# Routing a gated cross-attention block with experts: counts by TensorE, tile places by partition, expert weights split ahead of the last FFN pieces

## The chip, the cores and the metric

One core of one Trainium2 chip runs the whole program. The metric is the device time of one execution in microseconds (us), lower is better; of the kernel before three runs are given, and one profiled execution.

## What is computed

The input `x` has 32 samples of 256 tokens with 256 features, the context 32 times 77 tokens. Cut to what matters:

```python
x = x + tanh(g_xattn) * (attention(layernorm(x), ctx, ctx) @ W.T + b)      # 16 heads of 16, causal, softmax over 77
flat = layernorm(x)                                                        # 8192 tokens
shared = swiglu(flat @ w_in.T) @ w_out.T                                   # hidden 512
g_idx = argmax(flat @ wg.T + gb)                                           # 2 groups
masked = where(group of expert == g_idx, flat @ we.T + eb, -inf)           # 4 experts of that group
topv, topi = top_k(softmax(masked) * g_prob, 2)
routed = sum over the two: (swiglu(flat @ w1.T) * topv) @ w2[topi].T
x = x + tanh(g_ffn) * (shared + routed)
```

## The kernel before

A token's two experts lie in one group of four, so there are 2 x 6 = 12 pairs, called classes. **Phase one** goes over the samples: attention, the shared FFN and, from the logits, each token's class, its two weights and its place among the tokens of its class. GpSimd scatters a record (token, two weights) to that place in a table in DRAM (`tab`); the residual and the normed row go to `y` in DRAM. **Phase two** takes the table in tiles of 128 tokens of one class (`NTILE` = 76 at most, in chunks of four): GpSimd gathers their rows of `y`, TensorE transposes them, computes the hidden layer and multiplies it with the class's two experts, picked by a register; VectorE adds, GpSimd scatters the result.

The order of work is one Python list (`phase_one()`), which every engine's program walks through in the same sequence, emitting only its own part. Each iteration `i` has 12 slots into which the attention stages of several samples are put. Behind each slot come pieces of the shared FFN: a chunk of two samples has 24, of which 0 to 15 compute the hidden layer (four blocks: two pieces for `ha`, two for `hb`) and 16 to 23 the output, in halves `so`; pieces 19 and 23 end in `res`, which SyncE writes to `y`. Behind each FFN piece come pieces of a route. `ROUTES` lists nine: seven of eight tiles, two of four. A route of eight tiles has 63 pieces before: 55 for VectorE (each a small operation that waits for the one ahead) and 8 scatters for GpSimd. On the way a running count per class (`Cc`) is made tile by tile, and TensorE turns it and the one-hot classes (`OH`) into each token's rank (`rank`, L647 and L648).

TensorE's results go to rings of PSUM banks (`take`): the FFN and the rank share ring F with two banks in phase one and get ring B with all eight from `phase_two` on. A bank is free when its reader has counted a semaphore (`freed`): `u` and `f` for the hidden pieces, `res` for the output, `roh` (VectorE's product of rank and one-hot) for the rank. In hidden blocks ScalarE makes a tanh and a rounded copy `gh`, VectorE `u` (L1149) and `f` (`gf`, L1157), GpSimd the remainder `gl` (L1358), for which the output pieces wait.

At the end of phase one, `tiles` computes for each of the 76 tiles where it begins in the table (`ti`) and its experts (`ei`), on one partition of VectorE in 24 pieces (L1255 to L1289). `split_w2` turns the expert weights, loaded by SyncE in 16 halves into six buffers of `Pt`, into a rounded part (ScalarE) and a remainder (VectorE for even, GpSimd for odd halves), and issues the load that comes next. `records` has SyncE read a tile's place into a register and fetch its 128 records. `gather` has GpSimd fetch rows of `y`; it waits until all of `y` is written (`yr0`, `yr1`, `yn0`, `yn1`).

```python
            while at["ffn"] < (12 * (i - 5) + slot - 5) // 2 * 2:
                ...
                for _ in range(2 if i < NB else 3):
                    route()
```

Of the kernel before, what the change touches and what calls it, by code (L numbers as in the profile page):

```python
# [29 lines left out]
NCH = NB // 2  # L30


DCON = {n: i + 1 for i, n in enumerate(
    "idb ks0 kb0 ones rec pre_zero pre zero_row va_zero va_one wgh0 wgl0 tgh brow pbias".split())}
GCON = {n: i + 6 for i, n in enumerate("ident caus cauT upb".split())}
# [4 lines left out]
R_EXP1, R_EXP2, R_RANK = 3, 9, 30  # L40


def route_pieces(r):
    return R_RANK + 17 + 2 * ROUTES[r][1]
# [6 lines left out]
def phase_one():  # L51
# [15 lines left out]
    for i in range(NB + 4):  # L67
# [19 lines left out]
        for slot in range(12):  # L87
# [17 lines left out]
    n = w = tiles = 0  # L105
    while at["ffn"] < 24 * NCH:
        for _ in range(4):
            if at["r"] < len(ROUTES):
                route()
            elif tiles < 24:  # L110
                order.append(("tiles", 0, tiles))
                tiles += 1
        if n >= 4 and w < 2 * NE:
            order.append(("split_w2", w, 0))
            w += 1
        order.append(("ffn", at["ffn"] // 24, at["ffn"] % 24))
        at["ffn"] += 1
        n += 1
    while at["r"] < len(ROUTES):
        route()  # L120
    while tiles < 24:
        order.append(("tiles", 0, tiles))
        tiles += 1
# [6 lines left out]
def build(nc, A, out):  # L130
    ctx = ExitStack()
    with ctx:
# [3 lines left out]
            "xT mm mTp sc val O aT pj x2T lg lgt ha hb so rank tot z ha2 hb2 ex "  # L136
# [21 lines left out]
        def freed(use):  # L158
# [8 lines left out]
                "so": lambda: (s["res"], 2 * n + k + 1), "rank": lambda: (s["roh"], n + 1), "tot": lambda: (s["tv"], 1),  # L167
# [25 lines left out]
        Cc = sb("Cc", [P, 9, NC], BF)  # L193
# [4 lines left out]
        def carve(rows, shape, of=w2a):  # L198
# [61 lines left out]
        tb = sb("tb", [P, 2, 2, 512])  # L260
        tt, bt = tb[:, 0, :, :], tb[:, 1, :, :]
# [5 lines left out]
        LG = sb("LG", [P, 4, 4, 10])  # L267
        upb = sb("upb", [P, P], BF)
        io12 = sb("io12", [P, NC])
        l4 = sb("l4", [P, 8, 4])  # L270
        ge4 = sb("ge4", [P, 8, 4])
        s4t = sb("s4t", [P, 8, 4])
        c6 = sb("c6", [P, 8, 6])
        R1 = sb("R1", [P, 8, 8])
# [7 lines left out]
        half = NB // 2 * K  # L282
        mk_s = [v.bitcast(I32).rearrange("p (b k) -> p b k", k=K) for v in (
            af[:, 4736:4736 + half], tb[:, :, :, :].rearrange("p a b n -> p (a b n)")[:, 0:half])]
# [1184 lines left out]
```

## Time and profile before

| | |
|---|---|
| median of 3 runs | 1304.08 us (1302.39 to 1304.59) |
| the profiled execution, its own time | 1309.0 us |
| its span in the profile | 1307.2 us |
| TensorE busy | 1155.2 us (88% of the span) |
| VectorE busy | 865.0 us (66%) |
| GpSimd busy | 549.1 us (42%) |
| ScalarE busy | 505.8 us (39%) |
| mean granted TensorE clock | 0.969 of full speed |

Busy is the time in which an engine executes; an engine with 88% has some 150 us in which it does nothing, and the profile says for each such gap on whom it waited. In the profile's timelines and groups PE is TensorE, DVE VectorE, ACT ScalarE, POOL GpSimd, and SPq the DMA issues of SyncE. The granted clock is a share of 2.4 GHz; 0.5 is its lower level, 1.2 GHz.

### The profile page before, as it was taken

How to read it: one execution, taken by the hardware profiler on the slowest of the kernel's cores; microseconds unless marked ns; L12 is line 12 of the kernel's file. 1: busy time of each engine (PE TensorE's matmuls, PEld its weight loads, DVE VectorE, ACT ScalarE, POOL GpSimd, SP SyncE). 2: the span in 40 equal slices, each digit the busy share in tenths (PEclk: the TensorE clock that was granted, in tenths of full speed). 3: DMA queues.
4: the chain of work that ended last, by engine and by line, in shares of the span. 5: the costliest groups of instructions: out<-in, count | busy, mean ns of one | idle time of the engine just before them, and what ended most of it. 6: DMA issues, size and time to landing. Idle time of an engine off the chain costs nothing.

```text
span 1307.2 us, 22394 instructions
## 1 busy us (share of the span) xinstructions
PE 1155.2 (88%) x7387; PEld 918.4 (70%) x7387; DVE 865.0 (66%) x1968; ACT 505.8 (39%) x780; POOL 549.1 (42%) x658
## 2 busy tenths in 40 slices
PE   1688999998999999999999985179999999999997
PEld 0356777776777777777767764168888888888886
DVE  4455687687577777876876776546666566666665
ACT  3355555454455545554554423122222222222220
POOL 2122334326126235334342345345556556555543
PEclk9998999999999999999999988689999999999999
DMA  4756464645446355544635114323222222122210
GB/s 153 137 110 124 104 131 79 115 109 97 90 104 119 82 112 114 105 92 111 129 70 99 43 33 121 106 51 75 64 66 68 66 69 70 62 69 73 63 34 10
DMA packets 108263, 115.30 MB, mean 88 GB/s; under 512 B 36942, under 2 KB 88433, under 8 KB 108148
## 3 DMA queue, kind: packets, MB, share of 16 engines
q1 hardware_dynamic: 96376, 85.41, 31.6%
q0 software_dynamic: 11776, 28.46, 7.3%
q8 instruction: 64, 1.05, 0.4%
q14 instruction: 47, 0.39, 0.1%
HBM read 50.44 MB, written 28.64 MB: 60 GB/s over the span
## 4 chain that ended last, share of the span: by engine, by line
PE 64%; DVE 16%; issue 5%; POOL 4%; SPq 4%; DMA 3%; ACT 2%; POOLq 0%; DVEq 0%; ACTq 0%
PE ps L681 15%; PE ps L699 11%; PE ps L618 6%; PE ps L702 5%; PE ps L635 5%; PE ps L526 4%; PE ps L541 4%; PE ps L572 2%; PE ps L502 2%; DMA w2a<-w2a 2%; PE ps L497 2%; PE ps L594 2%; DVE mneg L1093 2%; PE ps L550 1%; DVE gf L1157 1%
## 5 line engine op out<-in xcount | busy, mean ns | idle before, releaser
L699 PE MATMUL ps<-w2a,gh 128*128 x608 | 218.5, 399 | 0.0
L759 ACT ACTIVATE Pt<-ps,pbias 77x1024 f32<-77x1024 f32 x128 | 142.1, 1110 | 103.3 <-PE ps L528 102.2
L702 PE MATMUL ps<-w2a,gl 128*128 x608 | 170.5, 280 | 0.0
L1411 POOL DMA_INDIRECT out<-ot,Pt x76 | 78.4, 1032 | 153.0 <-DVE ot L1232 149.6
L1303 POOL TENSOR_SCALAR ve<-mv 128x2 f32<-128x2 f32 x64 | 15.5, 242 | 284.7 <-DVE mv L882 284.0
L699 PEld LDWEIGHTS ps<-w2a,gh 128*128 128x128 f32 x608 | 114.2, 188 | 25.1
L1093 DVE TENSOR_REDUCE mneg<-ps 128x8 f32<-128x616 f32 x128 | 101.5, 794 | 44.6 <-PE ps L502 44.4
L681 PE MATMUL ps<-z2h,w1h 128*128 128x512 f32 x304 | 121.8, 401 | 8.3 <-DVE z2l L886 8.3
L1358 POOL TENSOR_TENSOR gl<-gf,gh 128x512 fp32r<-128x512 f32 x64 | 83.0, 1297 | 109.6 <-ACT gh L801 109.5
L526 PE MATMUL ps<-w2a 100*77 100x256 f32 x512 | 106.5, 324 | 22.9 <-DMA w2a<-w2a 17.9
L855 ACT ACTIVATE tt<-ps 128x512 f32<-128x512 f32 x76 | 45.4, 597 | 198.5 <-PE ps L681 198.5
L681 PE MATMUL ps<-z2l,w1h 128*128 128x512 f32 x304 | 120.5, 397 | 0.0
L681 PE MATMUL ps<-z2h,w1l 128*128 128x512 f32 x304 | 120.4, 396 | 0.0
L702 PEld LDWEIGHTS ps<-w2a,gl 128*128 128x128 f32 x608 | 114.5, 188 | 1.5
L618 PE MATMUL ps<-x2h,winh 128*128 128x512 f32 x256 | 112.7, 440 | 1.5 <-DVE gf L1157 1.3
L1397 POOL TENSOR_TENSOR gl<-gf,gh 128x512 fp32r<-128x512 f32 x76 | 98.5, 1297 | 16.4 <-ACT gh L859 14.5
L635 PE MATMUL ps<-woh,gh 128*128 128x256 f32 x256 | 79.9, 312 | 25.2 <-POOL gl L1358 25.1
L618 PE MATMUL ps<-x2h,winl 128*128 128x512 f32 x256 | 101.4, 396 | 0.0
L618 PE MATMUL ps<-x2l,winh 128*128 128x512 f32 x256 | 100.8, 394 | 0.0
L859 ACT ACTIVATE gh<-gf 128x512 fp32r<-128x512 f32 x76 | 48.0, 632 | 126.8 <-DVE gf L1215 126.8
L1210 DVE SCALAR_TENSOR_TENSOR uu<-tt,ps 128x512 f32<-128x512 f32 x76 | 52.2, 687 | 62.4 <-ACT tt L855 62.4
L526 PEld LDWEIGHTS ps<-w2a 100*77 100x77 f32 x512 | 64.2, 156 | 34.4 <-issue 21.1
(205 smaller groups left out, 2763.4 us busy)
## 6 DMA issues: line engine op xcount, KB each, us to landing
w2a<-w2a SPq DMA_DIRECT2D x96, 256.0 KB, 5.9
af<-in_x SPq DMA_DIRECT2D x32, 256.0 KB, 3.5
x<-in_x SPq DMA_DIRECT2D x32, 256.0 KB, 7.1
y_dram<-xn SPq DMA_DIRECT2D x32, 256.0 KB, 3.6
y_dram<-res SPq DMA_DIRECT2D x32, 256.0 KB, 2.4
w2a<-w2a SPq DMA_DIRECT2D x96, 77.0 KB, 2.8
Pt<-in_w2T SPq DMA_DIRECT2D x16, 256.0 KB, 3.5
af<-in_ctxT SPq DMA_DIRECT2D x16, 154.0 KB, 3.0
```

Source lines behind the costliest of these rows:

```text
L526: e.matmul(bk[0:K, j * S:(j + 1) * S], Kst[:, ks, j, p % 4, 2 * g + p // 4, :], Xs[:, h, p % 4, p // 4, :], start=j == 0, stop=False, skip ...
L541: m = e.matmul(bk[32 * j:32 * j + 32, q * S:(q + 1) * S], Vau[:, ks, g, n, :], Pt[0:K, n, :], start=True, stop=True)
L618: m = e.matmul(bk[:, :], w[:, cc, off:off + P], x[:, b % 2, cc, :], start=cc == 0 and n == 0, stop=cc == 1 and n == 2)
L635: m = e.matmul(o[:, t, :], x[:, fc, at:at + P], w[:, fc, :], start=fc == 0 and t == 0 and n == 0, stop=fc == 3 and n == 2, skip_group_chec ...
L681: m = e.matmul(bk[:, :], w[:, cc, off:off + P], x[:, c % 2, cc, :], start=n == 0, stop=n == 5)
L699: e.matmul(o, gh2[:, c % 2, fc, t * P:(t + 1) * P], w2v[:, bass.ds(val, 1), fc, :, :].rearrange("p o h d -> p (o h) d"), start=fc == 0, st ...
L702: m = e.matmul(o[:, 0, :], gl2[:, c % 2, fc, t * P:(t + 1) * P], w2v[:, bass.ds(val, 1), fc, 0, :].rearrange("p o d -> p (o d)"), start=Fa ...
L759: e.activation(Pt[0:K, 4 * k:4 * k + 4, :].rearrange("k (n j) t -> k n (j t)", n=2), bank_of["sc", b, k][0:K, :, :], ACT.Exp, bias=pbias[: ...
L1093: e.tensor_reduce(mneg[:, h, t, :].rearrange("p (j q c) -> p c j q", j=2, c=2)[:, c], bank_of["mm", b, k][:, :, 0:4 * K].rearrange("p q (f ...
L1358: e.tensor_tensor(gl[:, fc - 1, :], gf[:, n % 2, :], gh[:, fc - 1, :].bitcast(F), ALU.subtract).then_inc(s["gl"], 1)
L1397: e.tensor_tensor(gl2[:, c % 2, fc, :], gf2[:, fc % 2, :], gh2[:, c % 2, fc, :].bitcast(F), ALU.subtract).then_inc(s["gl2"], 1)
L1411: e.indirect_dma_start(out.rearrange("b s d -> (b s) d"), bass.IndirectOffsetOnAxis(ap=rt[:, k, 0:1].bitcast(I32), axis=0), ot[:, k % 8, : ...
```

## The change

- A route has 30 pieces for VectorE (32 instructions but for shared copies) and its scatters. Both groups' experts are compared at once (`cmp`, 4 x 4 comparisons per group) and masked by group (`gm`). The running count is one vector per route (`carry`, two buffers).
- The counts of tiles within a route are TensorE's: the rank sum gets one matmul of ones with the one-hot classes for each distance between tiles, one with the carry, one with the class's start in the table (`crow`), 10 matmuls for eight tiles and 6 for four.
- `tiles` has three pieces, with a tile on each partition: a matmul gives the totals per class (T1), one the running sum of tiles (T2), and three transposes (T3) bring place and experts back to one row.
- FFN pieces come nine slots later; one route piece stands behind each up to iteration 30, three after that. The scatters so get one FFN piece each.
- The first six loads of `w2` stand at the end of iteration 33 (`load_w2`), 12 of 16 splits in iteration 35, the last four among pieces 8 to 11 of the last FFN chunk.
- `sel` is gone; its numbers come with `io12`. The mask is loaded in parts of 19 and 13 samples. `LG` is split into `LGg` and `LGe`.

```diff
-            while at["ffn"] < (12 * (i - 5) + slot - 5) // 2 * 2:
+            while at["ffn"] < (12 * (i - 5) + slot - 14) // 2 * 2:
                 order.append(("ffn", at["ffn"] // 24, at["ffn"] % 24))
                 at["ffn"] += 1
-                for _ in range(2 if i < NB else 3):
+                for _ in range(1 if i < NB - 1 else 3):
                     route()
+            if i == NB + 3:
+                order.append(("split_w2", slot, 0))
+        if i == NB + 1:
+            order.append(("load_w2", 0, 0))
...
     order.append(("phase_two", 0, 0))
-    n = w = tiles = 0
+    n, w, k = 0, 12, 0
     while at["ffn"] < 24 * NCH:
-        for _ in range(4):
-            if at["r"] < len(ROUTES):
-                route()
-            elif tiles < 24:
-                order.append(("tiles", 0, tiles))
-                tiles += 1
-        if n >= 4 and w < 2 * NE:
-            order.append(("split_w2", w, 0))
-            w += 1
+        for _ in range(3):
+            route()
         order.append(("ffn", at["ffn"] // 24, at["ffn"] % 24))
         at["ffn"] += 1
         n += 1
+        if at["r"] == len(ROUTES) - 1 and at["k"] > R_RANK + 3 or at["r"] == len(ROUTES):
+            if n % 2 == 0 and k < 3:
+                order.append(("tiles", 0, k))
+                k += 1
+            elif k == 3 and w < 2 * NE:
+                order.append(("split_w2", w, 0))
+                w += 1
...
-                elif stage_ == "route" and k == R_RANK + ROUTES[b][1] + 6:
+                elif stage_ == "route" and k == R_RANK:
...
-                    e.matmul(bk[:, 0:J * NC], upb[:, :], OH[:, 0:J, :].rearrange("p j c -> p (j c)"), start=True, stop=False)
-                    e.matmul(bk[:, 0:J * NC], onesb[:, :], Cc[:, 0:J, :].rearrange("p j c -> p (j c)"),
-                             start=False, stop=True).then_inc(s["rank"], 1)
+                    o = OH[:, 0:J, :].rearrange("p j c -> p (j c)")
+                    e.matmul(bk[:, 0:J * NC], upb[:, :], o, start=True, stop=False, skip_group_check=True)
+                    for d in range(1, J):
+                        e.matmul(bk[:, d * NC:J * NC], onesb[:, :], o[:, 0:(J - d) * NC], start=False, stop=False,
+                                 skip_group_check=True)
...
+                elif stage_ == "tiles":
+                    bk, (sem, v) = take("B", ("T1", "T2", "T3")[k], 0, 0)
+                    e.wait_ge(sem, v)
+                    if k == 0:
+
+                        e.wait_ge(s["rcc"], len(ROUTES))
+                        e.matmul(bk[0:NC, 0:P], carry[:, len(ROUTES) % 2, :], onesb[:, :], start=True, stop=True).then_inc(s["T1"], 1)
+                    elif k == 1:
+
+                        e.wait_ge(s["nt"], 3)
+                        e.matmul(bk[:, 0:NC], ntb[:, :], upb[0:NC, 1:NC + 1], start=True, stop=True).then_inc(s["T2"], 1)
+                    else:
+                        e.wait_ge(s["tk"], 7)
+                        for n in range(3):
+                            m = e.transpose(bk[0:1, n * P:(n + 1) * P], tk[:, n:n + 1], ident[:, :])
+                        m.then_inc(s["T3"], 1)
...
-                for j in range(J):
-                    after()
-                    step(e.tensor_tensor(Cc[:, j + 1, :], Cc[:, j, :], OH[:, j, :], ALU.add), *(("rcc", r + 1) if j == J - 1 else ()))
+                step(e.tensor_reduce(ct[:, :], oh.rearrange("p j c -> p c j"), AX, ALU.add))
+                yield
+                after()
+                step(e.tensor_tensor(carry[:, (r + 1) % 2, :], ct[:, :], carry[:, r % 2, :], ALU.add), "rcc", r + 1)
```

What moves, at three places. First TensorE in the third route, at the rank sum (L647 and L648 before, L662 to L669 now; L618 and L631 are hidden pieces of the FFN, L635 and L648 of the change output pieces). Before:

```order
L618 MATMUL ps<-x2h,winl 128x512
L647 MATMUL ps<-OH,upb 128x96 [waits s_rcc,s_u]
L648 MATMUL ps<-Cc,onesb 128x96
L618 MATMUL ps<-x2h,winh 128x512
L618 MATMUL ps<-x2l,winh 128x512
L618 MATMUL ps<-x2h,winl 128x512
```

Now:

```order
L648 MATMUL ps<-woh,gl 128x256
L662 MATMUL ps<-OH,upb 128x96 [waits s_rcc,s_f]
L664 MATMUL ps<-OH,onesb 128x84
L664 MATMUL ps<-OH,onesb 128x72
L664 MATMUL ps<-OH,onesb 128x60
L664 MATMUL ps<-OH,onesb 128x48
L664 MATMUL ps<-OH,onesb 128x36
L664 MATMUL ps<-OH,onesb 128x24
L664 MATMUL ps<-OH,onesb 128x12
L666 MATMUL ps<-carry,onesb 128x96
L669 MATMUL ps<-crow,onesb 128x96
L648 MATMUL ps<-woh,gh 128x256 [waits s_gl]
```

The two sums have become ten matmuls, and stand between the output pieces 16 and 17, no longer in the middle of a hidden block.

Second, TensorE again, where the bank of that rank sum is next wanted (`s_roh` is VectorE's reading of it; L497 and L510 are score tiles of `max`). Before, in the next block of the same route's stretch:

```order
L526 MATMUL ps<-w2a 77x256 [waits s_mt0,s_P,s_xs0,s_kd0]
L526 MATMUL ps<-w2a 77x256
L528 MATMUL ps<-cauT,identb 77x2x77
L526 MATMUL ps<-w2a 77x256 x2
L528 MATMUL ps<-cauT,identb 77x2x77
L618 MATMUL ps<-x2h,winh 128x512 [waits s_roh]
L618 MATMUL ps<-x2l,winh 128x512
L618 MATMUL ps<-x2h,winl 128x512
```

Now, seven FFN pieces behind the sum, at the next chunk's piece 0:

```order
L541 MATMUL ps<-cauT,identb 77x2x77
L539 MATMUL ps<-w2a 77x256 x2
L541 MATMUL ps<-cauT,identb 77x2x77
L510 MATMUL ps<-w2a 128x308 [waits s_att]
L510 MATMUL ps<-w2a 128x308
L515 MATMUL ps<-pad,identb 128x308 x2
L631 MATMUL ps<-x2h,winh 128x512 [waits s_roh,s_x2l]
L631 MATMUL ps<-x2l,winh 128x512
```

The wait for `roh` has moved from behind the scores to right behind the score tiles of `max`, at hidden piece 0 of a chunk.

Third, VectorE at the end of phase one (`res` is the last FFN result, L1181 and L1186 splits, `w1l` the beginning of phase two). Before:

```order
L1181 TENSOR_TENSOR w2a<-Pt,w2a 128x2x256 [waits s_wh]
L1279 TENSOR_TENSOR Pt<-Pt 1x76 [waits s_tv]
L1280 TENSOR_TENSOR af<-af,Pt 1x912
L1282 TENSOR_REDUCE Pt<-af 1x76 [waits s_tv]
L1284 CAST af<-Pt 1x76 [waits s_tv]
L1285 TENSOR_TENSOR af<-af,Pt 1x912
L1287 TENSOR_REDUCE Pt<-af 1x76 [waits s_tv]
L1167 SCALAR_TENSOR_TENSOR res<-ps,tg,x 128x512 [waits s_yr1,s_x1,s_so]
L1289 TENSOR_SCALAR af<-Pt 1x76 [waits s_tv]
L1181 TENSOR_TENSOR w2a<-Pt,w2a 128x2x256 [waits s_wh]
L1196 TENSOR_TENSOR w1l<-Pt,w1h 128x4x128 [waits s_yn1,s_yn0,s_scat,s_yr1,s_wh,s_yr0,s_gl]
```

Now:

```order
L1287 TENSOR_SCALAR af<-ps 1x76
L1186 TENSOR_TENSOR w2a<-Pt,w2a 128x2x256 [waits s_wh]
L1154 SCALAR_TENSOR_TENSOR tt<-tt,ps 128x512 [waits s_t]
L1186 TENSOR_TENSOR w2a<-Pt,w2a 128x2x256 [waits s_wh]
L1162 TENSOR_TENSOR gf<-tt,ps 128x512 [waits s_gl,s_hb,s_u]
L1154 SCALAR_TENSOR_TENSOR tt<-tt,ps 128x512 [waits s_t]
L1162 TENSOR_TENSOR gf<-tt,ps 128x512 [waits s_gl,s_hb,s_u]
L1172 SCALAR_TENSOR_TENSOR res<-ps,tg,x 128x512 [waits s_yr0,s_x1,s_so]
L1172 SCALAR_TENSOR_TENSOR res<-ps,tg,x 128x512 [waits s_yr1,s_x1,s_so]
L1201 TENSOR_TENSOR w1l<-Pt,w1h 128x4x128 [waits s_yn1,s_yn0,s_scat,s_yr1,s_wh,s_yr0,s_gl]
```

The tile steps, now L1258 to L1287, end before the last two splits, and behind those only FFN rows are left; between the last two `res` there is nothing.

## Rows read from the trace of the kernel before

**Rows 1.** Windows, two steady iterations: PE, PEld, DVE, ACT, POOL busy, clock, DMA share, GB/s

```profile
446.10:466.30 20.20, 19.26 (x148) 14.66 (x146) 17.92 (x53) 11.98 (x20) 6.59 (x11) 1.00 0.52 116
490.10:511.80 21.70, 19.85 (x150) 14.89 (x148) 16.70 (x36) 11.92 (x19) 16.06 (x22) 1.00 0.56 114
```

**Rows 2.** Windows, the join of the two phases

```profile
750.00:770.00 20.00, 17.13 (x99) 14.07 (x98) 16.76 (x53) 5.57 (x11) 9.92 (x10) 1.00 0.06 16
770.00:780.00 10.00, 6.47 (x33) 5.71 (x32) 7.47 (x28) 1.23 (x2) 2.36 (x4) 0.67 0.15 52
...
790.00:800.00 10.00, 3.28 (x15) 2.35 (x13) 9.35 (x36) 4.49 (x10) 4.05 (x4) 0.87 0.27 81
800.00:810.00 10.00, 5.73 (x27) 4.94 (x27) 8.65 (x31) 4.94 (x10) 4.28 (x5) 0.79 0.53 167
810.00:820.00 10.00, 5.25 (x30) 5.05 (x30) 3.62 (x6) 1.89 (x3) 8.98 (x8) 0.66 0.40 93
...
870.00:880.00 10.00, 8.53 (x32) 6.98 (x33) 4.90 (x9) 3.04 (x6) 3.84 (x3) 0.71 0.07 2
```

**Rows 3.** Timeline of PE: start, us, engine, line, instruction, [idle before <-releaser]

```profile
800.19 0.20 PE L647 MATMUL ps<-OH,upb 128*128 128x48 bf16 x1 [6.92 <-DVE Cc L998]
...
814.60 0.58 PE L635 MATMUL ps<-woh,gh 128*128 128x256 f32 x1 [8.67 <-POOL gl L1358]
...
819.57 0.28 PE L635 MATMUL ps<-woh,gl 128*128 128x256 f32 x1
...
849.89 0.79 PE L681 MATMUL ps<-z2h,w1h 128*128 128x512 f32 x1 [1.41 <-DVE z2l L886]
...
871.47 0.79 PE L681 MATMUL ps<-z2h,w1h 128*128 128x512 f32 x1 [6.85 <-DVE z2l L886]
```

**Rows 4.** Timeline of POOL in the same stretch

```profile
812.05 1.27 POOL L1379 TENSOR_TENSOR w2a<-Pt,w2a 128x512 fp32r<-128x512 f32 x1
...
839.34 1.11 POOL L1294 DMA_INDIRECT af<-y_dram,Pt  x1 [19.85 <-DMA Pt<-tab_dram]
...
862.45 1.03 POOL L1294 DMA_INDIRECT yt<-y_dram,Pt  x1 [10.97 <-DMA Pt<-tab_dram]
```

**Rows 5.** Timeline of DVE: four route steps, a tile step, the last res

```profile
799.29 0.76 DVE L998 TENSOR_TENSOR Cc<-Cc,OH 128x12 bf16<-128x12 bf16 x4
...
821.12 1.10 DVE L1268 TENSOR_TENSOR af<-Pt 1x912 f32<-1x912 f32 x1
...
831.04 0.73 DVE L1167 SCALAR_TENSOR_TENSOR res<-ps,tg,x 128x512 f32<-128x512 f32 x1
```

**Rows 6.** Timeline of SyncE's DMA issues, merged

```profile
783.30 34.16 SPq L367 DMA_DIRECT2D Pt<-in_w2T  x16
...
831.80 0.38 SPq L439 DMA_DIRECT2D y_dram<-res  x1
833.44 46.01 SPq L378 DMA_DIRECT2D Pt<-tab_dram  x41
```

**Rows 7.** Timeline of ACT, its first row of phase two

```profile
834.21 0.63 ACT L841 ACTIVATE w1h<-Pt 128x512 fp32r<-128x512 f32 x1 [13.21 <-DMA y_dram<-res]
```

**Rows 8.** Windows, iterations 4 and 5, at the start of phase one

```profile
85.20:105.40 20.20, 13.22 (x106) 8.89 (x106) 10.26 (x25) 9.15 (x14) 3.84 (x8) 0.89 0.75 159
105.40:125.30 19.90, 19.37 (x136) 14.83 (x136) 11.67 (x26) 11.19 (x17) 4.96 (x9) 0.94 0.52 102
```

**Rows 9.** Chain that ended last: start, us; one hidden piece

```profile
781.71 1.38 PE ps L618 x6
```

**Rows 10.** By line: duration ns min/median/max, first and last start, forms

```profile
L647 PEld LDWEIGHTS ps<-OH,upb x9: 95/95/105, 206.6 to 800.2; 128*128 128x128 bf16 x9
...
L989 DVE TENSOR_TENSOR OH<-R,io x9: 207/247/257, 191.2 to 798.3; 128x96 bf16<-128x96 f32 x7, 128x48 bf16<-128x48 f32 x2
```

**Rows 11.** The page's groups: busy us, mean ns | idle before, releaser

```profile
L1093 DVE TENSOR_REDUCE mneg<-ps 128x8 f32<-128x616 f32 x128 | 101.5, 794 | 44.6 <-PE ps L502 44.4
```

**Rows 12.** Groups of PE from 100 to 700 us, same columns

```profile
L526 PE MATMUL ps<-w2a 100*77 100x256 f32 x428 | 86.1, 316 | 15.1 <-DMA w2a<-w2a 11.0 <-DVE mneg L1093 3.7 <-ACT Pt L759 0.4
```

More of the change, by code:

```diff
@@ L118, in phase_one @@
         n += 1
+        if at["r"] == len(ROUTES) - 1 and at["k"] > R_RANK + 3 or at["r"] == len(ROUTES):
[5 more added lines that the diff above has]
+                w += 1
     while at["r"] < len(ROUTES):
         route()
-    while tiles < 24:
-        order.append(("tiles", 0, tiles))
-        tiles += 1
+    order += [("tiles", 0, x) for x in range(k, 3)]
     order.append(("gather", 0, 0))
@@ L457, in sync @@
                         load_w(b + 6)
-                elif stage_ == "tiles" and k == 23:
+                elif stage_ == "tiles" and k == 2:
                     e.wait_ge(s["ti"], 1)
@@ L650, in tensor @@
+                    e.matmul(bk[:, 0:J * NC], onesb[0:1, :], crow[:, 0:J * NC], start=False, stop=True,
+                             skip_group_check=True).then_inc(s["rank"], 1)
                 elif stage_ == "phase_two":
                     ffn_ring = "B"
-                elif stage_ == "tiles" and k == 0:
-                    bk, (sem, v) = take("B", "tot", 0, 0)
+                elif stage_ == "tiles":
+                    bk, (sem, v) = take("B", ("T1", "T2", "T3")[k], 0, 0)
                     e.wait_ge(sem, v)
-                    e.wait_ge(s["rcc"], len(ROUTES))
-                    e.matmul(bk[:, 0:NC], onesb[:, :], Cc[:, ROUTES[-1][1], :], start=True, stop=True).then_inc(s["tot"], 1)
+                    if k == 0:
[9 more added lines that the diff above has]
+                        m.then_inc(s["T3"], 1)
@@ L927, in route @@
                 yield
                 after()
[L929 removed]
+                step(e.tensor_tensor(m_.rearrange("p t i j -> p t (i j)"), m_.rearrange("p t i j -> p t (i j)"), each(tri, T),
+                                     ALU.mult))
                 yield
                 after()
[L932 removed]
+                step(e.tensor_reduce(r_, m_, AX, ALU.add))
+                yield
+                step(e.tensor_reduce(c_, m_.rearrange("p t i j -> p t j i"), AX, ALU.add))
@@ L1019, in route @@
-                oh = OHR[:, 0:J, :]
-                step(e.tensor_tensor(oh, bank_of["rank", r, 0][:, 0:J * NC].rearrange("p (j c) -> p j c", c=NC), o, ALU.mult),
-                     "roh", r + 1)
-                yield
-                after()
-                step(e.tensor_reduce(col(5), oh, AX, ALU.add))
-                yield
+                for n, op in enumerate((ALU.is_lt, ALU.is_ge)):
+                    after()
+                    step(e.scalar_tensor_tensor(lh[:, :, n, :], by8(r_), 0.5, by8(e_), op, ALU.mult))
+                    yield
```

301 lines of the change are left out of this document (137 added, 164 removed), and 2 rows, old and new, of the table names.

## The prediction

> **What bounds the kernel now.** I read the busy time of the engines by stretch first, then TensorE's timeline where it is not full, then the timelines of the engines it waits for there. Phase one (attention, shared FFN and routing, to about 820 us) and phase two (the experts) both keep TensorE busy: two steady iterations of phase one show 19.26 of 20.20 us and 19.85 of 21.70 us [rows 1]. From 890 us to the end it is full, and the change touches nothing there. What is left is the join. From 750 to 820 us TensorE is idle for 2.87 + 3.53 + 6.72 + 4.27 + 4.75 = 22.1 us [rows 2]: most is a wait of 6.9 us for VectorE's class counts and one of 8.7 us for GpSimd's `gl` [rows 3], which stood behind record scatters and an expert split (`w2a` at 812.05) [rows 4]. The granted clock falls after such stops. Busy time times the missing share of the clock gives 6.5 x 0.33 + 3.3 x 0.13 + 5.7 x 0.21 + 5.3 x 0.34 = 5.6 us lost [rows 2]. Then comes the hole: the last FFN matmul starts at 819.6, the first hidden matmul of phase two at 849.9, 30.3 us later [rows 3]. In it VectorE works through the tile table on one partition in steps of 1.1 us, and the last `res` (done by the same engine) starts at 831.0 though its input was ready at 819.9 [rows 5]. SyncE writes it at 831.8, fetches records from 833.4 at 46.0 / 41 = 1.1 us each [rows 6], ScalarE sees the row landed at 834.2 [rows 7], GpSimd gathers from 839.3 [rows 4], and 10.6 us later TensorE is at work. Last, a stop of 6.9 us before 871.5 [rows 3], because the gathers of the third chunk wait for 24 records (862.5) and the `gl` of phase two stands behind them [rows 4].
>
> **The join after the change.** The order puts the end of routing, the three `tiles` pieces and the last four splits ahead of FFN piece 12 of the last chunk. Behind that only FFN work is left on VectorE and GpSimd. The eight records of the first two chunks are also fetched before the last `res`. So from the last FFN matmul on: 0.1 us to `res`, 3.2 us from its start to landed (831.04 to 834.21) [rows 5, 7], some 0.4 us to the gather, 10.6 us from gather to first hidden matmul [rows 3, 4]. That makes 14.3 us against 30.3: **-16.0 us**. Next is late the third chunk: SyncE starts its 16 records 1.6 us after the last `y` write (831.8 to 833.4), about 2.5 us behind the last matmul, so they are landed at 2.5 + 16 x 1.1 + 1.7 = 22 us; in the old run 9.0 us passed from that gather to TensorE (862.45 to 871.47) [rows 3, 4, 6]: 31.5 us. TensorE had run 14.7 us on its own before the old stop (871.5 - 6.9 - 849.9) [rows 3], so it now stops at 14.3 + 14.7 = 29.0 and waits 2.5 us instead of 6.9. The clock lost behind the old stop was 8.5 x 0.29 = 2.5 us [rows 2], of which I give back 2. Together **-6.4 us**.
>
> **The tail of phase one.** The 22.1 idle and 5.6 clock go, and new waits come, which I add as one term. TensorE waits in the last route for the counts (18 VectorE steps of 0.19 us and up [rows 5], with two `res` between, against 5.6 us of its own pieces): 2 to 4 us. T2 and T3 each want VectorE's answer after two FFN pieces (2.8 us): 2.5 together. `gl` of piece 19 is due 3.1 us after piece 15 and covered by 2.2 us: 1 each in chunks 14 and 15. Chunk 14 has splits in front of its `gl`: 2. I take **+10 us**, ends 4 and 22 (the last is what stands there now). Sum for the tail: **-17.7 us**.
>
> The splits themselves (12 in the last iteration of phase one) add per piece one ScalarE copy and half a split each on VectorE and GpSimd. They cost nothing while TensorE has a piece of 1.4 us beside each. The cover would be gone if the loads came no faster than the old 34.16 / 16 = 2.1 us each [rows 6]; those were paced by the order, not by the queue.
>
> **What it costs elsewhere.** (1) FFN pieces are issued nine slots later. Iterations without FFN take no less time: 20.2 us (85.2 to 105.4) with 13.2 busy, the next, with six pieces, 19.9 us with 19.4 busy [rows 8]. The filling starts later: by the end of iteration 6 the old order has 18 pieces out, the new 8. Eight of the ten missing are hidden pieces of 1.38 us [rows 9] and two are output pieces with half the columns, 0.7 us: 12.4 us of work falls out of a stretch with room into one without: **+12.4 us**. The bounds are 0 (iterations shorten as much) and 14. (2) Nine rank sums take 10 matmuls (6 for four tiles) for 2: 64 more, with at most 96 columns. From below they cost next to nothing, 1 us; from above the weight load, 95 ns each [rows 10], is 6 us. I take **+3**. The Trainium skill (TensorE: Matmul & The Clock Gate, "Back-to-back issue gap") gives about 81 ns for each pair of weight load and matmul with 128 columns; by that the term would be 5 us, and no row here times a run of such pairs.
>
> (3) The bank. Phase one has two banks for FFN and rank. Before, the rank sum was freed one route step after it was made. Now TensorE makes it at route piece 20, VectorE reads it at piece 28 (`roh`), one piece per FFN piece, so the hidden piece 0 of the next chunk waits for `s_roh`, just behind the score tiles of `max`. VectorE must first reduce those (0.79 us) [rows 11], then do the product (0.26 by the 96-element step) [rows 10]: 1.1 us in each of six routes, **+6.6**. (4) Against that the eight scatters of a route now stand one behind each FFN piece, no longer two. The iteration with scatters idles 1.85 us, the one without 0.94 [rows 1]: seven times 0.9 is **-6.4**. The queries' DMA before the scores gets a light or heavy pair more beside it; waits for it in the steady part are 11.0 us in all [rows 12], of which I take **-3**. VectorE loses about 23 instructions in a route of eight tiles and gains seven bigger ones: worth nothing, since it is not what the steady part waits for.
>
> **Sum.** -16.0 - 6.4 - 17.7 + 12.4 + 3 + 6.6 - 6.4 - 3 = -27.5 us. The profiled execution took 1309.0 us, so it would be 1281.5; the median of the runs is 1304.1, which gives **1277 us**.
>
> **Rivals.**
> A, the above: 0.53, from 1268 to 1284.
> B, the tail gives half of it back: splits and tanh share ScalarE with only two banks, or the records delay the last `y` write (SyncE must fetch eight of them, 8.8 us, after the last scatter has landed, and has only about 11 us of matmuls for it). For: GpSimd's scatters held everything up here before. Against: eight pieces without any side work follow. The tail term rises from 10 to 22, giving 1289. Chance 0.20.
> C, steady iterations gain too (idle 0.9 instead of 1.4 on average over 25 iterations, from scatters, lighter VectorE and better cover of the queries' DMA): about 13 us more, 1264. For: VectorE is 17.9 of 20.2 us busy there. Against: TensorE is 95% busy. Chance 0.17.
> D, slower: the bank of (3). VectorE is not just one reduction behind at piece 28 but also behind `klo`, which waits for ScalarE and a load, and each wait is long enough to bring the clock down. At 5 us of wait and 2 of clock, six times, the term is 42 for 6.6, giving 1312. It decides from 34 / 6 = 5.7 us per wait. For: it is a true wait with nothing of TensorE's that can pass it. Against: in the old trace VectorE is some 0.6 us behind at that slot. Chance 0.06.
> E, no change: the hole moves. The later filling (12.4), the bank and a tail as bad as before cancel what the hole gives, 1300 to 1306. The code does move the work, so this needs several at once: 0.04.
>
> **Numbers.** The likeliest case gives 1277. A reaches from 1268 to 1284, B above to 1292, C below to 1260: the range 1261 to 1291 leaves out about 2 in 10. Faster or slower counts beyond 0.2% (2.6 us, about what runs of this kernel can tell). Faster 0.90 (A, B, C), same 0.04 (E), slower 0.06 (D).
>
> **What would show it.** The last FFN matmul some 5 us earlier than 820; 14 to 15 us from there to the first hidden matmul, with the `y` write right behind `res`; the stop in phase two below 4 us; in the last route single waits below 4 us; FFN starting in the iteration that begins at 125 us with about 12 us more idle before; six waits of TensorE of about 1 us for `OHR`. I am wrong if waits for `OHR` are 4 us or more, if iterations before the first FFN piece get shorter than 19 us, or if `y` is written 3 us or more after `res`.

## The result and the profile after

The changed kernel took 1299.55 us (median of 20 runs, 1292.18 to 1306.12), the kernel before beside it 1306.2 us: ratio 0.9943, interval 0.9926 to 0.996. It is faster by some 7 us; 1277 was forecast, and the measured time lies above the forecast's 1261 to 1291. The profiled execution took 1304.0 us, span 1302.3.

The page of the changed kernel, busy time by engine and the granted clock in 40 slices:

```profile
PE 1157.2 (89%) x7455; PEld 918.1 (70%) x7455; DVE 814.9 (63%) x1767; ACT 502.4 (39%) x780; POOL 549.3 (42%) x659
...
PEclk9998999999999999999999998889999999999999
```

VectorE has 50 us less to do, TensorE as much as before. The join by windows (columns as in [rows 2]), with the two steady windows of [rows 1] at the end:

```profile
750.00:770.00 20.00, 19.23 (x147) 15.80 (x147) 9.18 (x23) 9.93 (x14) 13.91 (x15) 1.00 0.09 27
770.00:780.00 10.00, 7.97 (x58) 6.65 (x57) 9.02 (x34) 2.12 (x5) 0.94 (x2) 0.99 0.82 241
...
800.00:810.00 10.00, 5.94 (x29) 5.49 (x30) 8.53 (x16) 4.56 (x9) 7.67 (x6) 0.68 0.74 240
810.00:820.00 10.00, 8.53 (x45) 6.10 (x43) 8.31 (x34) 2.23 (x4) 1.14 (x1) 0.98 0.27 79
...
840.00:850.00 10.00, 1.08 (x4) 0.72 (x4) 0.74 (x1) 0.63 (x1) 4.93 (x5) 0.56 0.55 156
870.00:880.00 10.00, 10.00 (x52) 8.27 (x52) 5.39 (x10) 3.29 (x6) 4.86 (x5) 1.00 0.11 17
446.10:466.30 20.20, 19.23 (x163) 15.37 (x162) 12.77 (x36) 9.20 (x16) 5.66 (x10) 1.00 0.51 106
490.10:511.80 21.70, 18.16 (x158) 13.92 (x158) 12.38 (x37) 8.35 (x13) 5.47 (x10) 1.00 0.50 101
```

TensorE's timeline at the hole, against [rows 3]: the last FFN matmul, the first hidden one of phase two, the second stop.

```profile
836.62 0.28 PE L648 MATMUL ps<-woh,gl 128*128 128x256 f32 x1
848.92 1.09 PE L699 MATMUL ps<-ident,af 128*128 128x128 f32 x4 [12.02 <-DMA af<-y_dram,Pt]
...
854.51 0.80 PE L713 MATMUL ps<-z2h,w1h 128*128 128x512 f32 x1 [1.41 <-DVE z2l L918]
...
869.48 0.50 PE L713 MATMUL ps<-z2h,w1h 128*128 128x512 f32 x1 [1.07 <-DVE z2l L918]
```

The hole is 854.51 - 836.62 = 17.9 us (30.3 before), the second stop 1.1 (6.9). Yet the last FFN matmul starts 17.1 us later than before. Cut at four marks, both profiled executions:

| stretch | before | after | forecast | measured |
|---|---|---|---|---|
| start to ScalarE's norm of sample 31 | 691.6 | 709.65 | +0.2 | +18.0 |
| from there to the last FFN matmul | 128.0 | 127.0 | -5.3 | -1.0 |
| hole | 30.3 | 17.9 | -16.0 | -12.4 |
| first hidden matmul to the end | 457.3 | 447.8 | -6.4 | -9.5 |

In the first row, rank sums, bank, scatters and queries were put at +3 + 6.6 - 6.4 - 3 = +0.2; the second has 12.4 - 17.7. The miss is in the iterations, which took 18 us longer although some 12 us of FFN work had left them. What TensorE waited for there, 100 to 700 us (engine, line, releaser: us in total, times, longest). Before:

```profile
PE ps L635 <- POOL gl L1358: 11.1, 10, 1.5
PE ps L526 <- DMA w2a<-w2a: 11.0, 6, 5.2
PE ps L497 <- DVE mneg L1093: 10.0, 18, 0.8
PE ps L526 <- DVE mneg L1093: 3.7, 12, 0.4
```

After:

```profile
PE ps L563 <- ACT Pt L791: 17.2, 25, 1.0
PE ps L631 <- DVE OHR L1038: 13.9, 6, 2.3
PE ps L539 <- DMA w2a<-w2a: 11.8, 6, 6.0
PE ps L585 <- ACT af L798: 9.8, 25, 0.4
```

The waits for `gl` and for the maxima are gone; in their place stand one for ScalarE's exp and one for its copy ahead of the projection, 25 times each, and one for the rank's bank, 13.9 us where 6.6 were forecast. In all TensorE is idle for 55.3 us of these 600, before for 37.1. Timeline of PE in one iteration:

```profile
454.55 0.23 PE L541 MATMUL ps<-cauT,identb 77*77 77x154 bf16 x1
454.71 0.41 PE L510 MATMUL ps<-w2a 64*128 64x308 f32 x2
455.05 0.45 PE L515 MATMUL ps<-first,identb 128*128 128x308 bf16 x2
456.07 1.06 PE L563 MATMUL ps<-ident,af 128*128 128x128 f32 x8 [0.58 <-ACT Pt L791]
```

The transposes of attention (L563, slot 2) want the bank that the exp of the scores (slot 1) empties. The two FFN pieces that an iteration issues together are called a pair here. With `slot - 5` the pairs stood behind the odd slots, so one lay between scores and transposes; with `slot - 14` they stand behind the even ones, and none does. The same holds for values (slot 9) and projection (L585, slot 10). The shift by nine changed the parity, which the forecast didn't see.

### The profile page after: what moved, and what is told of

Its sections match the earlier page's. It is cut to its first block, busy times and chain, and to the rows that moved or that the text cites. A ratio compares the mean times of both kernels' runs of the same rounds, so it can differ in the third digit from the quotient of the medians.

```text
span 1302.3 us, 22338 instructions
## 1 busy us (share of the span) xinstructions
PE 1157.2 (89%) x7455; PEld 918.1 (70%) x7455; DVE 814.9 (63%) x1767; ACT 502.4 (39%) x780; POOL 549.3 (42%) x659
## 4 chain that ended last, share of the span: by engine, by line
PE 73%; ACT 6%; issue 5%; DVE 5%; SPq 5%; DMA 4%; POOL 2%; POOLq 0%; ACTq 0%; DVEq 0%
PE ps L713 15%; PE ps L731 11%; PE ps L631 10%; PE ps L648 6%; PE ps L734 6%; PE ps L539 4%; PE ps L554 4%; PE ps L585 3%; DMA w2a<-w2a 3%; PE ps L563 3%; ACT Pt L791 3%; PE ps L515 2%; PE ps L510 2%; PE ps L607 2%; PE ps L541 1%
## 5 line engine op out<-in xcount | busy, mean ns | idle before, releaser
L631 PE MATMUL ps<-x2h,winh 128*128 128x512 f32 x256 | 112.2, 438 | 15.3 <-DVE OHR L1038 13.9
L1301 POOL TENSOR_SCALAR ve<-mv 128x2 f32<-128x2 f32 x64 | 15.2, 237 | 254.7 <-DVE mv L914 254.3
L539 PE MATMUL ps<-w2a 100*77 100x256 f32 x512 | 99.1, 310 | 19.8 <-DMA w2a<-w2a 18.9
L1396 POOL TENSOR_TENSOR gl<-gf,gh 128x512 fp32r<-128x512 f32 x76 | 98.6, 1298 | 14.7 <-ACT gh L891 13.0
L631 PE MATMUL ps<-x2h,winl 128*128 128x512 f32 x256 | 102.1, 399 | 0.0
L631 PE MATMUL ps<-x2l,winh 128*128 128x512 f32 x256 | 101.5, 397 | 0.0
L1374 POOL DMA_INDIRECT tab_dram<-rec,slot x64 | 65.7, 1026 | 58.6 <-issue 56.2
```

The source lines that it names most:

```text
L539: e.matmul(bk[0:K, j * S:(j + 1) * S], Kst[:, ks, j, p % 4, 2 * g + p // 4, :], Xs[:, h, p % 4, p // 4, :], start=j == 0, stop=False, skip ...
L631: m = e.matmul(bk[:, :], w[:, cc, off:off + P], x[:, b % 2, cc, :], start=cc == 0 and n == 0, stop=cc == 1 and n == 2)
L1374: e.indirect_dma_start(tab, bass.IndirectOffsetOnAxis(ap=slot[:, j:j + 1], axis=0), rec[:, j, :], None, bounds_check=NC * NT - 1, oob_is_e ...
L1396: e.tensor_tensor(gl2[:, c % 2, fc, :], gf2[:, fc % 2, :], gh2[:, c % 2, fc, :].bitcast(F), ALU.subtract).then_inc(s["gl2"], 1)
```

## The experiments

The versions were timed in four groups, each on another chip and beside the kernel before, to which all ratios refer. Its median was 1310.8 us in the first group (the four below up to changed_odd_slots) and 1306.3 to 1307.6 in the others, so a difference between versions of two groups is better taken from the ratios; where that matters both are given. Odd and even name the slots that the pairs stand behind.

### The parity of the FFN slots

**before_even_slots**

```diff
-            while at["ffn"] < (12 * (i - 5) + slot - 5) // 2 * 2:
+            while at["ffn"] < (12 * (i - 5) + slot - 6) // 2 * 2:
```

> The kernel before with nothing changed but the shift of the FFN pieces, six slots instead of five, which puts its pairs behind even slots. Theory P: waits for ScalarE's exp (Pt) and its copy ahead of the projection appear in each iteration, some 0.6 and 0.4 us, over 32 iterations 15 to 30 us; time 1318 to 1335. Rival F: one slot less of filling is worth at most 2 us; 1306 to 1308.

1326.6 us, ratio 1.010 (1.006 to 1.014): 16 us slower. The waits appear, the first of them twice as long as expected (29.3 us in 25 waits):

```profile
PE ps L550 <- ACT Pt L759: 29.3, 25, 2.6
PE ps L572 <- ACT af L766: 11.1, 25, 1.0
```

**before_later_even** (`slot - 14` in the kernel before)

> The kernel before with the shift of the changed one (14 slots instead of 5) and nothing else of it. Some 12 us of FFN work move behind the last iteration, where before has 37 us of idle; if they all fill idle time the later filling costs nothing by itself. Theory P: the parity adds 15 to 30 us to the iterations and the tail gives nothing extra back; 1315 to 1330. Rival F: 1300 to 1308.

1340.3 us, 1.022 (1.018 to 1.025): 29.5 us slower, more than theory P's upper end. The same two waits stand in each iteration:

```profile
PE ps L550 <- ACT Pt L759: 18.0, 25, 1.0
PE ps L572 <- ACT af L766: 17.9, 25, 2.6
```

By the marks of the table above, the norm of sample 31 starts 30.5 us later (722.1), the last FFN matmul another 25.0 us later behind it (153.0 for 128.0), and the hole shrinks by 15.5 us (14.8 for 30.3).

**before_later_odd** (`slot - 13`)

> The kernel before with a shift of 13 slots, later by eight as the changed kernel nearly is, but on odd slots as before. Theory P: 15 to 25 us below the same kernel with 14 slots; against the kernel before between no change and 10 us faster (the displaced work fills the 30.3 us hole at the join), 1296 to 1306. Rival F: as with 14 slots, within 2 us.

1290.5 us, 0.983 (0.980 to 0.987). One slot between these two kernels makes 50 us, more than theory P said. And this one number alone, in the kernel before, is worth more than the whole change: the norm of sample 31 starts at 671.1, 20.5 us earlier; the last FFN matmul comes 22.0 us later behind it; the hole shrinks from 30.3 to 14.75 us, since VectorE's tile steps now lie beside FFN work. Of the 20.5 us, 17.0 lie between samples 8 and 31, where each iteration has six pairs in both kernels: the waits for `gl` (11.1 us) are gone there. After the hole:

```profile
835.80 0.80 PE L681 MATMUL ps<-z2h,w1h 128*128 128x512 f32 x1 [1.41 <-issue]
```

**changed_odd_slots** (`slot - 13` in the changed kernel)

> The changed kernel with its FFN pieces eight slots later than before instead of nine, so that pairs stand again behind the odd slots (1, 3, 5, 7, 9, 11) of an iteration and not behind the even ones. Theory P (parity): in the changed kernel PE's transposes of the attention weights (L563) wait 17.2 us and its projections (L585) 9.8 us in 100 to 700 us for ScalarE, 25 times each, because no pair stands between scores and transposes, nor between values and projection; with pairs there both waits go almost wholly, and the time is 15 to 27 us below the changed kernel's 1299.6, near 1280. Rival F (later filling alone): the 12 us that the iterations lost against before come from nine slots of FFN work that are not there in iterations 5 and on, and parity is nothing: 1299 to 1301. Rival R: the waits go, but PE then meets the next late thing of each iteration (max, DMA rows of maxT), and only 3 to 8 us are won.

1332.8 us, 1.016 (1.013 to 1.020): slower by 33 us than on even slots (29 by the ratios), against theory P and its rivals. The two waits for ScalarE did go, but others grew:

```profile
PE ps L539 <- DMA w2a<-w2a: 16.1, 7, 5.8
PE ps L631 <- DVE OHR L1038: 14.6, 5, 3.4
PE ps L595 <- DVE xn L1136: 12.0, 5, 2.4
```

The waiting is 48 us, less than the 55 on even slots; what is lost is clock: 0.94 from 100 to 400 and from 400 to 700 us, where the changed kernel has 0.96 and 1.00. Of stops of 1.5 us and more there are 14 here, and the granted clock is below 1.00 in the 3 us behind 13 of them; the changed kernel has seven, with a lower clock behind two. Behind one of them, PE's timeline and the window (clock is the third number from the end):

```profile
316.89 0.77 PE L631 MATMUL ps<-x2h,winh 128*128 128x512 f32 x1 [3.26 <-DVE OHR L1038]
317.46 0.63 PE L631 MATMUL ps<-x2l,winh 128*128 128x512 f32 x1
```

```profile
316.00:322.00 6.00, 5.11 (x16) 3.42 (x16) 2.25 (x6) 0.60 (x1) 0.35 (x2) 0.50 0.21 60
```

The matmuls take 0.63 us (0.39 otherwise): the clock is at its lower level. The Trainium skill (TensorE: Matmul & The Clock Gate, "Part 1: The HAM clock gate") has the clock fall when TensorE has been idle; this row agrees. How long a stop is does not settle it here: of the six waits of 2.3 us in the changed kernel one was followed by the lower clock in its first profile, and three in the profile of changed_once_more, the same program.

### The rank's bank

**changed_product_early**: VectorE's product, which frees the bank, six steps earlier.

```diff
+                e.wait_ge(s["rank"], r + 1)
+                e.tensor_tensor(OHR[:, 0:J, :], bank_of["rank", r, 0]..., oh, ALU.mult).then_inc(s["roh"], 1)
+                yield
                 after()
                 step(e.tensor_tensor(e_, e_, s_, ALU.mult))
...
-                e.wait_ge(s["rank"], r + 1)
-                step(e.tensor_tensor(OHR[:, 0:J, :], bank_of["rank", r, 0]..., oh, ALU.mult), "roh", r + 1)
-                yield
-                after()
+                e.wait_ge(s["roh"], r + 1)
                 step(e.tensor_reduce(cl[:, 0:J], OHR[:, 0:J, :], AX, ALU.add))
```

> The changed kernel (14 slots, even) with VectorE's product of the rank bank and the one-hot (L1038) six steps earlier, right behind the rank sums. Theory Q (the bank): the wait of 2.3 us at L631 that comes once with each of the six eight-tile routes of iterations 8 to 28 goes, and with it the half-speed clock behind it; 6 x 2.3 = 14 us of waiting and some 3 to 6 us of clock, so 1280 to 1288 against the 1299.6 of the changed kernel. Rival W: the FFN piece then waits for something else that is late at the same place (the copy of its own gate, the weights of attention), and 5 us or less are won.

1281.0 us, 0.9813 (0.979 to 0.984): 18.6 us below the changed kernel (17 by the ratios), as theory Q has it. The wait is gone, the others stay:

```profile
PE ps L563 <- ACT Pt L791: 18.6, 26, 1.0
PE ps L585 <- ACT af L798: 10.2, 26, 0.4
PE ps L539 <- DMA w2a<-w2a: 9.9, 6, 6.0
```

From sample 8 to 31 it needs 518.4 us for 536.1: 17.7, the 13.9 of waiting and 3.8 more, which fits the clock of 0.83 from 315 to 335 us, around the second stop. Why 2.3 us and not 1.1 shows VectorE's queue of the changed kernel ahead of one product:

```profile
506.30 0.48 DVE L1079 TENSOR_TENSOR w2a<-af,w2a 128x308 fp32r<-128x308 f32 x1 [0.78 <-ACT w2a L761]
506.70 0.79 DVE L1097 TENSOR_REDUCE mneg<-ps 128x8 f32<-128x616 f32 x1
507.41 0.25 DVE L1038 TENSOR_TENSOR OHR<-ps,OH 128x96 f32<-128x96 f32 x1
```

```profile
507.80 0.47 PE L631 MATMUL ps<-x2h,winh 128*128 128x512 f32 x1 [2.32 <-DVE OHR L1038]
```

The remainder of the keys (L1079, rival D's `klo`) waits 0.78 us for ScalarE and takes 0.48, then the maxima: 1.1 us more in front of the product than counted.

**changed_odd_product_early**: both edits.

> The changed kernel with its FFN pieces behind odd slots (13) and the product early. On odd slots, without the early product, the profile showed once with each eight-tile route a wait of 2.3 to 3.4 us for the product (L631 for DVE L1038) and one of 2.4 us for the normed rows (L595 for DVE xn, which waits for GpSimd's root behind the scatters), and a clock of 0.94. Theory Q: the first of the two goes, 15 to 20 us of waiting and half of the lost clock; 1332.8 falls to 1305 to 1315. Theory C (the rare long stops cost through the clock, the short ones of each iteration nothing but themselves): the same, and the clock between 100 and 700 us rises from 0.94 to 0.96 or 0.97. Rival: the clock stays at 0.94 whatever stops are left; then over 1315.

1290.3 us, 0.9867 (0.984 to 0.989): 42 us below the same slots without it (38 by the ratios), more than theory Q said, clock 0.97 in both halves. On odd slots the wait for the normed rows (L595, 9.7 us) and the DMA's (17.5) are left.

### How the routing is spread

**changed_odd_early_two_steps**

```diff
-                for _ in range(1 if i < NB - 1 else 3):
+                for _ in range(2 if i < NB - 1 else 3):
                     route()
```

> As the run on odd slots with the product early, and with two steps of routing to an FFN piece instead of one, as the kernel before has it; the eight scatters of a route then lie within four FFN pieces, not eight. Theory S: the wait for the normed rows (L595) came from GpSimd's root standing behind single scatters that were spread over the slots 7 to 11; with the scatters together it is gone in most routes, and with both long stops gone the time is that of the kernel before with 13 slots (1290.5 beside 1310.8 of before, 0.983) less the 10 us of the shorter join; 1270 to 1285. Rival: with two steps to a piece the product has half the distance from the rank sums, or VectorE's steps crowd out the maxima; 1290 to 1310.

1279.8 us, 0.9808 (0.978 to 0.983).

**changed_even_early_two_steps** (the same with `slot - 14`)

> The run with the product early and two steps of routing to an FFN piece (1279.8 on odd slots), now on even slots (14). Nothing but the parity differs. Theory P: the waits for ScalarE between scores and transposes and ahead of the projection (18.6 and 10.2 us in 100 to 700 us of the even run with one step) come back and nothing else goes; 1300 to 1310. Rival G (the parity only exchanges one set of late work for another: on odd slots PE is ahead of the maxima and of the DMA rows, on even slots of ScalarE): 1278 to 1288. With one step to a piece even was 9 us faster than odd.

1294.8 us, 0.9922 (0.989 to 0.995): between what theory P and rival G gave. The waits for ScalarE did come back (19.3 and 10.2 us), and the parity is worth 15 us here. On even slots one step is better by 13.8 (with two, GpSimd's `gl` is late behind pairs of scatters: 8.6 us of waits), on odd slots two by 10.5 (8 by the ratios; with one, the scatters stand among GpSimd's square roots, and the normed rows are late). The spread and the parity can't be valued apart.

**changed_scatters_behind_root**. In the odd run with two steps TensorE still waits twice for the normed rows around the last samples. PE, then POOL, whose eight scatters (six ahead of the root at L1301 and L1303) hold it up:

```profile
725.91 1.08 PE L595 MATMUL ps<-ident,xn 128*128 128x128 f32 x4 [5.32 <-DVE xn L1136]
...
769.40 1.09 PE L595 MATMUL ps<-ident,xn 128*128 128x128 f32 x4 [7.12 <-DVE xn L1136]
```

```profile
716.30 1.13 POOL L1374 DMA_INDIRECT tab_dram<-rec,slot  x1 [1.51 <-DVE slot L1044]
...
722.83 0.97 POOL L1374 DMA_INDIRECT tab_dram<-rec,slot  x1 [0.30 <-issue]
723.81 0.26 POOL L1301 TENSOR_SCALAR ve<-mv 128x2 f32<-128x2 f32 x1
```

```diff
+        if at["k"] == R_SCAT and at["d"] < {6: 8, 7: 8}.get(r, 0):
+            at["d"] += 1
+            return
...
     while at["ffn"] < 24 * NCH:
-        for _ in range(3):
+        for _ in range(5):
             route()
```

> As the run on odd slots, product early, two steps; and the scatters of the last two routes inside the iterations start only behind GpSimd's root of the attention norm (they stood ahead of it; PE's transposes L595 waited 5.3 us at 725.9 and 7.1 us at 769.4 for the rows normed with it), with five steps instead of three to a piece behind the last iteration, so that the last route isn't later. Theory S: both waits go, 12 us, part of it given back at the join if that is bound by the last scatters; 1268 to 1275. Rival: the join is bound by the records that follow the last scatters and by the last FFN rows; what PE wins earlier it waits there; 1277 to 1281.

**1268.9 us, 0.9714 (0.969 to 0.974)**, 30.7 us below the changed kernel, the fastest but for a tie below. The waits of L595 behind 700 us fell from 12.4 to 2.1 us. Norm of sample 31 at 669.95, last FFN matmul 129.4 us later, hole 17.8.

### The join

**changed_write_ahead_of_records**. SyncE's issues in the changed kernel: eight records, four loads of `w1`, then the last two rows of `y`.

```profile
828.14 8.55 SPq L393 DMA_DIRECT2D Pt<-tab_dram  x8
836.79 2.53 SPq L387 DMA_DIRECT2D Pt<-in_w1T  x4
839.38 1.10 SPq L454 DMA_DIRECT2D y_dram<-res  x2
```

```diff
                     records(0)
-                    records(1)
...
+                elif stage_ == "gather":
+                    records(1)
```

> The changed kernel with the loads of the second group's records (4 of the 8 small ones that SyncE issues ahead of the join) moved behind the last two writes of y. In the changed kernel the eight took 8.55 us from 828.1 and the writes of y were issued at 839.4, some 2.5 us after the last FFN rows were ready. Theory J: the writes go 2 to 3 us earlier, so does everything behind the join; 1297. Rival: the write waits for the rows themselves and the w1 loads, nothing changes (1299.6), or the second group's records come late for its gather and PE waits there for up to 4 us more.

1304.4 us, 0.9975 (0.995 to 1.000): no gain. The changed kernel took 1299.6 us and, in its second set of runs below, 1303.4, so this is not clearly slower either. The hole did close as theory J says, 835.94 to 850.62, 14.7 us for 17.9; but from there to the end it took 454.8 us for 447.8, and the stop behind the hole grew from 1.1 to 6.4 us:

```profile
850.62 0.80 PE L714 MATMUL ps<-z2h,w1h 128*128 128x512 f32 x1 [1.41 <-DVE z2l L919]
870.93 0.80 PE L714 MATMUL ps<-z2h,w1h 128*128 128x512 f32 x1 [6.36 <-DVE z2l L919]
```

SyncE fetches one record in 1.1 us, and the third chunk needs all twelve; what is put behind the write comes later there. That this makes the stop is argued from the order of the fetches; no run moves them alone.

**changed_scatters_root_write_first**: the fastest version with the last four `w1` loads and the third chunk's records behind the writes.

> As the run before it, and SyncE's order at the join changed: the last two writes of y go ahead of the last four loads of w1, and the third group's records follow the writes, ahead of those loads. The writes were issued 2 us behind the last FFN rows. Expected 1 to 3 us below the run before it. Rival: the second half of w1 is late for the first hidden layer and PE waits there for 3 us or more; no gain or slower.

1274.7 us, 0.9756 (0.973 to 0.978), 6 us slower. The hole is 16.1 us (805.3 to 821.4) for 17.8, but the profile is 4.6 us behind already at sample 4, where the two programs are the same. From the norm of sample 31 to the end it takes 596.5 us for 595.0: what the hole gained was lost again behind it, where the second stop is 2.5 us for 1.6. The order at the join won nothing.

### A price and the start

**rank_sums_repeated**

```diff
-                    e.matmul(bk[:, 0:J * NC], upb[:, :], o, start=True, ...)
+                    for _ in range(33):
+                        e.matmul(bk[:, 0:J * NC], upb[:, :], o, start=True, ...)
```

> The changed kernel with the product early (1281.0), and the first of the matmuls of the rank sums issued 33 times instead of once in each of the eight routes (same bank, same result), 256 more of them. The forecast put 3 us on the 64 matmuls and 64 weight loads that the change adds, some 47 ns each. If PE is the bound all along and each costs its time on the engine, 256 more cost 12 us: 1293. Rival: they fall into waits (each route's 32 in one place, against 1 to 2 us of waiting per iteration), then 4 us or less; or they reach the product and the bank, and the long stop comes back: 1300.

1296.6 us, 0.9913 (0.989 to 0.994), 15.6 above the kernel it was made from (13 by the ratios). There are nine routes, not eight, so 288 more: some 45 to 54 ns each, 3 to 3.5 us for the 64 of the change. TensorE's own rows agree: a run of 33 takes 1.41 us, 43 ns each; in the changed kernel the ten matmuls of a rank sum take 0.53 us from the first start to the next output piece (210.48 to 211.01), where the two of before took 0.08 (206.65 to 206.73), 56 ns for each of the eight more. The Trainium skill's 81 ns for such a pair (TensorE: Matmul & The Clock Gate, "Back-to-back issue gap") is for 128 columns, here there are 96 and fewer; by it the 288 would cost 23 us, an estimate, and the measurement decides for less.

**changed_once_more**: no edit.

> The changed kernel itself, once more, unchanged. Its first profile reached iteration 4 at 87.92 us, the kernel before at 85.17, the other twelve between 82.0 and 88.4, with no order by what was changed in them. Theory V (the first 90 us vary from execution to execution by some 6 us, whatever the kernel): this profile reaches iteration 4 somewhere else in 82 to 88 us, 0.5 us or more from 87.92. Rival K (the larger load of the constants and the uneven parts of the mask make the start later): again 87.5 to 88.4. The time within 1297 to 1304.

1303.4 us, 0.9964 (0.994 to 0.999). Sample 4 starts at 83.8 (87.9 in the first profile), sample 31 at 710.45 (709.65). So the start varies by itself, theory V, and the 18 us of the iterations don't come from it: an earlier start was lost again. Kernels that differ by 4 us in one profile can't be told apart by that.

**best_rows_loaded_first**: SyncE loads the first two samples ahead of the masks.

> The fastest version so far (1268.9: odd slots, product early, two steps, scatters behind the root), with SyncE's loads of the first two samples ahead of the mask and the weights instead of behind. VectorE's first moments wait 6 us for them in the changed kernel. Expected: the first norm of ScalarE 1 to 3 us earlier than 22.3 us and the time 1 to 2 us lower, 1267; rival: the mask or the first keys come later instead and the scores of sample 0 start when they did; 1268.9, no difference.

1269.4 us, 0.9704 (0.967 to 0.973). The first norm starts at 18.15 instead of 22.3, and the time is the same: at sample 4 only 1.1 of the 4.2 us are left. The rival holds.

## Why the prediction was wrong

**The step that failed: the later filling, (1) of what it costs elsewhere, +12.4 with bounds 0 and 14.** It took the shift of the FFN pieces as 12.4 us of work that moves to the end, and the steady iterations as bound by TensorE's own work, so that they keep their length. The kernel before with the same shift and nothing else was 29.5 us slower (before_later_even), and with one slot less 20.3 us faster (before_later_odd): both outside the bounds, on either side. Between samples 8 and 31, where every iteration keeps its six pairs, the first took 34.6 us more than before and the second 17.0 less. What counts is not how much work moves but which FFN pair stands between a producer and its consumer. With nine slots none is left beside ScalarE's exp and its copy. The forecast had no term for these two waits per iteration; they came to 17.2 and 9.8 us in the changed kernel.

The profiles of before, before_later_even (the shift alone) and the changed kernel split the change into this shift and everything else, in us:

| stretch | before | shift alone | changed | shift | the rest |
|---|---|---|---|---|---|
| start to the norm of sample 31 | 691.6 | 722.1 | 709.65 | +30.5 | -12.5 |
| from there to the last FFN matmul | 128.0 | 153.0 | 127.0 | +25.0 | -26.0 |
| hole | 30.3 | 14.8 | 17.9 | -15.5 | +3.1 |
| first hidden matmul to the end | 457.3 | 450.8 | 447.8 | -6.5 | -3.0 |
| span | 1307.2 | 1340.7 | 1302.3 | +33.5 | -38.4 |

The forecast had +12.4 for the shift and -39.9 for the rest. So nearly the whole miss of 22.6 us (-27.5 forecast, -4.9 measured between these two profiles) is the shift. That the rest agrees in sum is in part luck, since its terms do not, as the next paragraphs show. The split holds for this order of the two edits: the runs show that the parity is worth something else on other tables.

**The reading behind it.** Rows 8 set an iteration with no FFN, 20.2 us, beside one with six pieces, 19.9. The first is one at the start, with a clock of 0.89. In the changed kernel the iteration before the first FFN piece took 18.9 us, below the 19 us that the forecast had named as a sign of being wrong.

**The parity.** The formula was read as nine slots of delay; which stages lose the pair behind them was looked at for the bank only, not for ScalarE. On the tables of the kernel before it costs 16 us at five or six slots and 50 at thirteen or fourteen; on the changed ones, with the early product and two steps, 15. In the changed kernel as it stands even slots are the better ones. Both parities meet the late product there (13.9 and 14.6 us of waits); what the odd slots alone have is the late normed rows (12.0 us) and the clock of 0.94. Why the clock falls so much more often there the runs don't show.

**The bank, +6.6.** Mechanism right, six waits of TensorE for the product, but 2.3 us each and not 1.1. Freeing it early won 17.7 us between samples 8 and 31, so the term was 11 us too small. Rival D named the reason (`klo` ahead of the product, then the clock) and set its price too high: the sign held.

**The scatters, -6.4.** With the product early and even slots one step per piece is worth 13.8 us, on odd slots it costs 10.5. These runs change the pace of the whole route, not the scatters alone. The gain existed on the slots that were made, at up to twice the size.

**The rank sums, +3.** Measured 3 to 3.5.

**The tail, -17.7.** The stretch fell by 1.0 us, and by 5.3 in the forecast. The waits that were listed came: counts 0.8 to 1.6 us, T3 1.5, `gl` 3.6 + 2.7 + 2.1, and the window from 800 us at a clock of 0.68. By the table the shift lengthened it by 25.0 us, not by 12.4, and routing, tiles and splits took 26.0 off. The waits and their cause were right, both sizes too small. One part of rival B held (GpSimd and the splits made `gl` late once by 3.6 us). Between before_later_odd and the fastest version, which have the same 13 slots and reach sample 31 within 1.1 us, the tail is 150.0 and 129.4 us.

**The hole, -16.0.** Measured -12.4. From gather (843.86) to hidden matmul it took 10.65 us as said. But from the start of the last `res` (836.94) to the landed row (843.08) it took 6.1 us, not 3.2, because the write stood behind eight records and the `w1` loads: rival B's mechanism, at a smaller price. The forecast's 14.3 us is what stood there once part of the records stood behind the write (14.7). And what the forecast took as the work of the new `tiles` is reached by the shift alone, with the old ones (14.8).

**The second stop, -6.4.** Measured 1.1 us instead of 2.5, -9.5 in all. The shift alone gives 6.5 of it.

Rival E gave this time, 1300 to 1306, with the later filling and the bank among its causes, but it had the tail as bad as before and the hole moved; the tail was 26.0 us better than with the shift alone, and the hole did shrink. Right were the places of the gain and what happens at the join. The sign held by little, 33.5 us lost against 38.4 won, and that is luck. Wrong was that the steady part, 600 us of the program, stays as it is: it was counted by work, not by what stands between a producer and its consumer.

## What to carry to other kernels

When a table shifts filler work against a fixed pattern of stages, write down for each wait in the pattern which filler covers it before and after; a shift by one slot made 50 us where the work was the same. When a ring's bank is shared by two uses, put its reader right behind its writer in the reader's program: six steps in the wrong place cost 18.6 us. And test the shift by itself in the old kernel first: with thirteen slots it gave more than the change, with fourteen it took four times what the change gave.

## What was not expected of the hardware

Total waiting does not tell the loss: 48 us of waits with 14 stops of 1.5 us and more left a clock of 0.94, 55 us with seven such stops 0.96 and 1.00. The same stop of 2.3 us, at the same place of the same program, was followed by the lower clock once in six times in one execution and three times in another. Two executions of one program started sample 4 at 83.8 and 87.9 us, and the times of one kernel spread over 1292 to 1310 us. A first norm that started 4.2 us earlier changed nothing in the end.
